# A gated two-layer block on one core: GpSimd issues the gathers of the second attention behind the transposed scores

## The reference, cut to what matters

```
x = x + tanh(g_xattn[0]) * cross_attention_0(layernorm(x), ctx)      # 8 heads of 64
x = x + tanh(g_ffn[0])   * experts(layernorm(x))                     # top 2 of 16 experts per row
x = x + tanh(g_xattn[1]) * cross_attention_1(layernorm(x), ctx, ctx) # 16 heads of 8, 77 keys
x = x + tanh(g_ffn[1])   * (fp8(bf16(layernorm(x))) @ fp8(kernel) + ffn_bias)
```

## Time and profile before

| | us |
|---|---|
| median of 3 runs | 1195.06 (1191.57 to 1212.96) |
| the profiled execution's own time | 1195.27 |
| its span | 1193.4 |
| PE busy | 1052.4 (88%) |
| DVE busy | 822.2 (69%) |
| POOL busy | 648.9 (54%) |
| ACT busy | 588.0 (49%) |
| gathers, POOL L598, 128 of them | 128.7, 1005 ns each |

### The profile page before, as it was taken

One profiled execution on the slowest core, in us unless ns is written; L12 is line 12 of the kernel. 1 busy time (PEld: TensorE's weight loads), 2 busy tenths in 40 slices (PEclk: granted clock), 3 DMA queues, 4 the chain that ended last, 5 costly groups with the idle time before them and its releaser, 6 DMA issues. The chain is left out here.

```text
span 1193.4 us, 41254 instructions
## 1 busy us (share of the span) xinstructions
PE 1052.4 (88%) x13498; PEld 848.3 (71%) x13499; DVE 822.2 (69%) x2573; ACT 588.0 (49%) x1415; POOL 648.9 (54%) x1155
## 2 busy tenths in 40 slices
PE   4999999979999993898899996899999999998893
PEld 4788787856877772677777784677777777776672
DVE  1777777786777776444444445678888888887784
ACT  2666666644656651334344441335555454544454
POOL 2333333324777776666620004467777777777755
PEclk9999999998999997899999997999999999999997
DMA  3321122222334201244343332111111111111101
GB/s 73 86 50 43 38 52 69 68 66 70 98 90 104 70 23 39 86 125 122 111 112 88 88 88 58 32 29 36 43 41 45 40 45 39 45 41 40 41 23 31
DMA packets 106888, 74.21 MB, mean 62 GB/s; under 512 B 21360, under 2 KB 98288, under 8 KB 106736
## 3 DMA queue, kind: packets, MB, share of 16 engines
q1 hardware_dynamic: 98544, 55.40, 17.9%
q0 software_dynamic: 8192, 16.79, 4.7%
HBM read 38.60 MB, written 33.55 MB: 60 GB/s over the span
## 5 line engine op out<-in xcount | busy, mean ns | idle before, releaser
L659 ACT ACTIVATE arena<-PS 77x512 f32<-77x512 f32 (+4 forms) x736 | 305.1, 441 | 464.5 <-PE PS L1177 270.7
L1177 PE MATMUL PS<-arena 128*32 128x128 f32 (+5 forms) x9488 | 452.9, 291 | 50.2 <-issue 16.6
L1177 PEld LDWEIGHTS PS<-arena 128*32 128x32 f32 (+4 forms) x9488 | 352.4, 145 | 129.4 <-issue 36.5
L1177 PE MATMUL PS<-w,arena 128*128 x960 | 199.8, 325 | 9.0 <-issue 7.1
L521 POOL DMA_INDIRECT moe_rows<-arena x128 | 127.4, 996 | 71.7 <-POOL arena L517 50.3
L1177 PEld LDWEIGHTS PS<-w,arena 128*128 128x128 f32 x960 | 135.5, 195 | 29.8 <-issue 17.8
L640 POOL TENSOR_TENSOR arena<-arena,minus_half 128x2 f32<-128x2 f32 (+1 forms) x71 | 51.2, 721 | 189.4 <-DVE arena L1156 185.5
L598 POOL DMA_INDIRECT arena<-moe_results,slot x128 | 128.7, 1005 | 43.8 <-issue 31.6
L536 POOL TENSOR_TENSOR arena<-arena,minus_half 128x2 f32<-128x2 f32 (+1 forms) x70 | 47.6, 680 | 187.9 <-DVE arena L834 166.4
L1057 DVE TENSOR_TENSOR arena<-PS,b_rows 128x256 f32<-128x256 f32 x160 | 67.8, 424 | 90.0 <-PE PS L1177 74.4
L1177 PEld LDWEIGHTS PS<-arena,wk_wq 128*128 128x128 f32 x512 | 80.4, 198 | 45.5 <-issue 43.0
(11 more groups left out here) (151 smaller groups left out, 1657.9 us busy)
## 6 DMA issues: line engine op xcount, KB each, us to landing
moe_rows<-zeros SPq DMA_DIRECT2D x64, 160.0 KB, 2.5
arena<-moe_rows SPq DMA_DIRECT2D x40, 256.0 KB
moe_results<-arena SPq DMA_DIRECT2D x40, 256.0 KB
residual<-in_x SPq DMA_DIRECT2D x64, 64.0 KB
w<-in_W SPq DMA_DIRECT2D x32, 128.0 KB
arena<-in_ctxC SPq DMA_DIRECT2D x64, 64.0 KB
out<-arena SPq DMA_DIRECT2D x64, 64.0 KB, 1.6
arena<-in_ctxT SPq DMA_DIRECT2D x32, 77.0 KB
```

The costliest lines, as they stand in the source:

```text
L659: A.activation(o, i, ACT.Copy).then_inc(s[done], 1)
L1177: return T.matmul(o, l, r, start=start, stop=stop)
```

## The change: gathers last, bias first, and a wait

On GpSimd, in each step of stage C, the addition of the FFN bias moves ahead of the gathers, and the first gather also waits until TensorE has finished the transposed scores of the same step. No instruction is added or taken away otherwise.

```
-                if (b := t.at(0)) is not None:
-                    gather(b, t.par(0), t.chunk)
                 if (b := t.at(15)) is not None:
                     p = t.par(15)
                     pool.wait_ge(s["y4_made"], b + 1)
                     wait_free(pool, s["obs_made"], b - 1)
                     g.tensor_tensor(y4b[p], y4[p], fbias[:, :], ALU.add).then_inc(s["y4b_made"], 1)
+                if (b := t.at(0)) is not None:
+
+                    wait_free(pool, s["ST_mm"], t.seen(6, 1))
+                    gather(b, t.par(0), t.chunk)
```

## The result

| | before | after |
|---|---|---|
| median, us | 1193.42 (4 runs, 1191.57 to 1212.96) | 1233.83 (4 runs, 1231.73 to 1237.14) |
| ratio to before | | 1.035, 95% interval 1.031 to 1.038 |
| span of the profiled execution, us | 1193.4 | 1230.4 |
| a typical step of stage C, us | 6.69 | 7.42 |

I had forecast 1187 us and a range that ended at 1213. A step came out at 7.42 us where I had 6.65. The ratio leaves out the execution of 1212.96 us, which ran in a slower state.

What follows compares the result with a forecast made beforehand. The prediction took a loop of waits to bound stage C. At 6.65 us a step, 345.5 and 28.4 us become 339.2 and 26.6, 8.1 less, giving 1187 us; range 1178 to 1213.

Steps and rivals of the forecast that it cites:

- the term +2.35: Stage C, GpSimd: the first gather starts 2.35 us after the step's first score matmul, instead of 1.82.
- the floor: Stage C: loop of transposed scores, gathers, rounding, transposition and scores; 6.27 + 0.22 = 6.49 us, the least a step takes.
- VectorE's loop: Stage C: denominators' signal held to about +5.28, then 1.40 us from reciprocal to scores, a step of 6.68 us.
- The key projection's signal not held: Stage C, TensorE to VectorE: the signal falls into the first gather, yet L1105 has no idle time, as in step 44.
- rival 1: Stage C: key projection's signal held as today, L1105 at +4.38, a step of 7.05 us, 1209 us; chance 0.27.
- rival 2: Stage C: key projection's signal held through both gathers, L1105 at +5.26, a step of 7.93 us, 1258 us; chance 0.09.
- The second gather 1.37 behind the first: Stage C, GpSimd: the second gather starts 1.37 us behind the first, at +3.72.
- The denominators' signal held to 1.56 behind the second gather: Stage C, TensorE to VectorE: the signal comes 1.56 us behind the second gather's start, at about +5.28.
- Moving the bias free: Stage C, GpSimd: the moved FFN bias takes 0.4 us but costs nothing while the wait ends later than +2.2.
- Rival 3: Stage C: the late signal has another cause than the gathers; wait ends at +3.12, loop 7.41 us, 1229 us; chance 0.07.
- Landing hidden: Stage C, the gathers' DMAs: L1078 uses the data 3.2 us after the second gather begins, so landing costs nothing.
- The rule: By the skill's sentence gathers cannot delay TensorE's signal; the prediction sided with the trace, ScalarE's wait 0.92 us longer beside a gather.

Runs made afterwards that it cites:

- The wait ahead of the bias: The changed kernel with its new wait moved one instruction up, ahead of the FFN bias: 1222.03 us, ratio 1.060 to the kernel before.
- the fills: Each gather replaced by a constant fill on GpSimd: in the kernel before 1144.16 us against 1153.28, in the changed kernel 1158.62 us.

## Why the prediction was wrong

**The step that failed** is the start of the first gather, the term +2.35 that both loops of the prediction are built on: "A gather starts some 0.17 us after what precedes it ... so I put the first at +2.35". The 0.17 is the gap behind a running instruction. Behind the new wait, when that is met last, it is 0.77 to 0.79 from ScalarE's start, in the four profiles with the wait right ahead of the gather and in all their steps from 12 to 63 but two, which have 1.08. So the first gather was at +2.98. A row that shows it was in the trace that I had read. Stage A's scatter is the same kind of instruction behind a met wait:

```profile
529.02 0.30 POOL L517 COPY arena<-slot 128x1 int32 x2
530.09 0.98 POOL L521 DMA_INDIRECT moe_rows<-arena  x1 [0.78 <-POOL arena L517]
```

The wait ahead of the bias showed that the time is the gather's and not the signal's, and the fills that it is not the wait's. With +2.98 in place of +2.35 the floor is 7.12 and VectorE's loop, by my own terms, 7.31. I took a gap from rows in which the queue never stood still, for a place where the change makes it stand still.

**The other terms.** The wait is met at +2.2: right, +2.21. The key projection's signal not held: right, +3.16, no idle time; rival 1 and rival 2 fell. The second gather 1.37 behind the first: 1.53, since the first takes 1.22 us and not 1.06. I had named a changed length as a sign of being wrong; why it is longer in this profile, and 1.06 on the second chip, stays open. The denominators' signal held to 1.56 behind the second gather: 1.49. From the reciprocal to the scores 1.40: 1.41. Moving the bias free: it is (GpSimd idles 0.18 ahead of the met wait), and with the bias left behind the gathers the wait costs 1.080 on the first chip rather than 1.060 on the second. The four differences, +0.63, +0.16, -0.07 and +0.01, are the 0.73 between the 6.68 of that loop and 7.41.

**Rival 3** gave 7.41 us and 1229, nearly what was measured, for the wrong reason: it had the transposed scores' signal late at +3.12, and that signal is on time at +2.21. Its number is no evidence for it.

**Landing hidden.** In the changed kernel's first profile L1080 waits for data once in 220 us. On the second chip it waits in most steps, 0.8 us each, in this answer on who VectorE waits for (us in total, times, longest), from 860 to 1080:

```profile
DVE arena L1080 <- DMA arena<-moe_results,slot: 21.5, 27, 1.9
```

Nothing is held there, so VectorE is through with its step earlier and comes to L1080 1.8 us behind the second gather's start (923.62 against 921.83), not the 3.2 that I had reckoned with. The wait costs nothing all the same: behind it VectorE still idles for L642 (0.48 us in this step), and the next scores wait for L631. So my zero for the cost held in both profiles, but the cover that I gave as its reason was there in one only.

**The rule.** I had weighed "PE and ACT never wait on anyone" (the Trainium skill, SBUF — State Buffer, section "Who interferes with whom") against the rows and held that the trace disagrees. Both can be had: on the first and second chip ScalarE's wait ends at +2.20 beside a running gather, in the two profiles of the kernel before with a time near 1194 us it ends at +3.12 to +3.15. The rule as a statement on ports may stand. As a forecast of whether TensorE's signals come on time beside an indirect DMA it holds on two chips and fails on a third and in the first profile.

The size of the loss depends on this. From step 12 to 63 the changed kernel takes 381.7 us in its first profile and 382.0 on the second chip, the kernel before 345.5 and 319.0. So 1.035 and 1.060 differ through the kernel *before*: where signals are held it already loses 27 us, and part of the new loop is hidden under that. That 381.7 and 382.0 agree so well is chance: typical steps are 7.42 and 7.27 us, and the long scores' rows add 1.6 us to the one and some 10 to the other.

**Open.** Why TensorE stops beside a gather on some chips. In the rows it issues nothing for 0.3 to 0.4 us at a time in the run of small matmuls, `<-issue` (945.44 in the changed kernel, 1007.91 and 1004.79 on the third chip), and its signals come late. The fills exclude GpSimd's being busy as the cause; the writing of the gather's descriptors, its data, and TensorE's supply of instructions were not told apart.

## What to carry to other kernels

In these runs an indirect DMA on GpSimd has some 0.8 us between its met wait and its first recorded instant. Hide it: let its wait be met while other work is still running on that queue, or put a short instruction between wait and gather. The FFN bias ran there for nothing; that gains time only where the instruction costs some in its old place. Before a wait is added in front of such a transfer, look for an instruction of the same kind that already stands behind a met wait, anywhere in the trace, and take its gap. Then close the loop on paper: scores, wait, start-up, gathers, rounding, scores. And profile the kernel before on more than one chip when a mechanism rests on late signals.

## What the hardware showed that I had not expected

- The same kernel took 1153.3 and 1153.5 us on two chips and 1194.8 on a third, each within a few us over seven to ten runs. Of the 41 us, 27 lie in the steps from 12 to 63, typically 6.16 against 6.70 us each, and 13 ahead of them (the first gather of step 12 starts at 771.14 on the second chip, at 784.01 on the third).
- A gather's preparation runs beside a compute instruction of the same queue: 0.72 us from the start of the bias to the gather, with 0.42 us of addition inside it. The Trainium skill, Perfetto Trace Analysis, section "DMA Instruction — SWDGE (GPSIMD)", says that the profiler has no start marker for a DMA whose descriptors GpSimd makes; by that, the start that the rows do give cannot be taken as the moment at which its cost begins. The rows agree as far as they go: 0.8 us of nothing, then 1.06 us of gather.
- After waits of 1.56 to 1.58 us on TensorE in each of four steps the granted clock was 0.63 over 4 us, and 56 rows of scores took 3.06 instead of 2.14 us; ahead of the fourth it was 1.00.
- The releaser's name can mislead. On the second chip 47.6 us ahead of the gathers are put down to VectorE's L1102 and 45.6 to TensorE, over stage C, but the gather starts 0.8 us behind the transposed scores' signal whichever is named: L1102 starts at +2.56 in the step of 924.74 and at +3.55 in that of 940.22, the gather at +2.99 and +2.98.
